# Cross-attention and FFN layer on one core: scales by PE and on-chip moves, K and V products one by one, and three kinds of transfer on ACT's queue

## The reference, cut to what matters

```
x = x + xattn(layernorm(x), ctx, mask, wq, bq, wk, bk, wv, bv, wo, bo)   # 16 batches, 112 rows, width 512; 375 context rows
x = x + ffn(layernorm(x), W1, B1, W2, B2)                                # hidden width 2048

xattn:  q = quantized_linear(x, wq) + bq        # rows of x and of wq scaled to integers up to 127
        k = ctx @ wk.T + bk ;  v = ctx @ wv.T + bv        # float32
        attn = softmax(q k.T / sqrt(32) + mask)           # 16 heads of 32
        o = attn @ v ;  out = quantized_linear(o, wo) + bo
ffn:    quantize rows, matmul with quantized W1, + B1, gelu, quantize rows, matmul with quantized W2, + B2
```

## Time and profile before

| | us |
|---|---|
| median of 3 runs | 748.97 (744.27 to 751.18) |
| the profiled execution, whole | 753.85 |
| its span, first to last instruction | 751.9 |
| mean granted clock of PE | 0.941 |
| busy: PE, DVE, ACT, POOL | 633.2, 469.8, 444.6, 300.4 |

### The profile page before, as it was taken

The page is one execution under the profiler, slowest core; times in us unless marked ns, Lnnn a source line. Parts: engine busy times, 40 slices in busy tenths (PEclk is TensorE's granted clock), DMA queues, the critical chain, the costliest instruction groups (busy, mean ns, idle before and its releaser), DMA issues.

```text
span 751.9 us, 14564 instructions
## 1 busy us (share of the span) xinstructions
PE 633.2 (84%) x4936; PEld 474.4 (63%) x4986; DVE 469.8 (62%) x1101; ACT 444.6 (59%) x1085; POOL 300.4 (40%) x555
## 2 busy tenths in 40 slices
PE   1838779979797799989699899989897999998763
PEld 1736566857665576767668677867675686766421
DVE  6635667856774295667376665468554576856763
ACT  2316555757763384949369566668584587878400
POOL 4232433453544353545452444353461333231231
PEclk9988898998998899999899999999999999999967
DMA  9985297752324425451722525324323112201321
GB/s 290 254 87 129 69 173 182 231 90 67 59 51 79 45 40 100 34 95 39 68 72 38 99 17 111 52 49 39 98 52 67 35 36 54 55 24 13 64 49 42
DMA packets 92664, 61.07 MB, mean 81 GB/s; under 512 B 69952, under 2 KB 79936, under 8 KB 91952
## 3 DMA queue, kind: packets, MB, share of 16 engines
q1 hardware_dynamic: 92592, 60.15, 41.2%
HBM read 42.09 MB, written 3.69 MB: 61 GB/s over the span
## 4 chain that ended last, share of the span: by engine, by line
PE 43%; DMA 21%; DVE 11%; SPq 9%; issue 8%; POOL 5%; ACT 1%; DVEq 0%; POOLq 0%
PE ps_ring L869 10%; PE ps_t L889 7%; PE ps_ring L855 7%; DMA oqT<-o_q 5%; PE ps_ring L933 5%; DMA q_dram<-cols 4%; PE ps_s L880 4%; PE ps_ring L945 4%; PE ps_t L902 4%; SPq L344 3%; DMA hT<-h_q 3%; DMA yqT<-y_q 2%; DMA xT<-x_q 2%; DMA q_dram<-so_col 1%; DMA b_row<-in_w2T 1%
## 5 line engine op out<-in xcount | busy, mean ns | idle before, releaser
L577 ACT ACTIVATE probs<-probs,neg_max 112x375 f32<-112x375 f32 x256 | 153.6, 602 | 36.5 <-DVE neg_max L702 36.0
L587 ACT ACTIVATE pT<-ps_t 125x336 f32<-125x336 f32 x256 | 109.0, 446 | 93.3 <-PE ps_t L889 91.6
L702 DVE CUSTOM_DVE_ANT_0 probs<-ps_s,mask_in 112x375 f32<-112x375 f32 x256 | 127.0, 543 | 56.4 <-PE ps_s L880 49.0
L889 PE MATMUL ps_t<-ident,probs 112*125 112x112 f32 x768 | 149.5, 287 | 4.4 <-ACT probs L577 2.1
L889 PEld LDWEIGHTS ps_t<-ident,probs 112*125 112x125 f32 x768 | 125.3, 199 | 36.9 <-issue 17.2
L855 PE MATMUL ps_ring<-ctx_hi,wk_hi 128*128 128x376 f32 x256 | 95.6, 373 | 29.0 <-DVE wk_lo L608 15.8
L869 PE MATMUL ps_ring<-wv_hi,ctx_hi 128*125 128x512 f32 x192 | 86.3, 449 | 2.1 <-issue 2.0
L855 PE MATMUL ps_ring<-ctx_lo,wk_hi 128*128 128x376 f32 x256 | 87.8, 343 | 0.0
L855 PE MATMUL ps_ring<-ctx_hi,wk_lo 128*128 128x376 f32 x256 | 87.6, 342 | 0.0
L463 POOL TENSOR_TENSOR ctx_lo<-ctx_in,ctx_hi 128x376 fp32r<-128x376 f32 x64 | 66.7, 1068 | 49.7 <-ACT ctx_hi L557 48.8
L945 PE MATMUL ps_ring<-w_q,hT 128*128 128x512 bf16 x207 | 65.9, 417 | 19.0 <-DMA hT<-h_q 18.2
(11 more groups left out here) (107 smaller groups left out, 1071.4 us busy)
## 6 DMA issues: line engine op xcount, KB each, us to landing
ctx_in<-in_ctxT SPq DMA_DIRECT2D x32, 375.0 KB, 6.3
h<-in_w2T SPq DMA_DIRECT2D x4, 1024.0 KB, 9.0
b_row<-in_w2T SPq DMA_DIRECT2D x4, 1024.0 KB, 9.8
xres<-in_x SPq DMA_DIRECT2D x14, 256.0 KB, 2.8
x_in<-in_x SPq DMA_DIRECT2D x16, 224.0 KB, 4.3
out<-y SPq DMA_DIRECT2D x14, 256.0 KB, 2.7
mask_in<-in_mask SPq DMA_DIRECT2D x16, 164.1 KB, 3.9
w_q<-in_w1T SPq DMA_DIRECT2D x2, 1024.0 KB, 13.9
```

Source lines behind the costliest of these rows:

```text
L577: nc.scalar.activation(probs[:, hd % SP_RING, :], probs[:, hd % SP_RING, :], ACT.Exp, scale=-1.0, bias=neg_max[:, b % 2, hd:hd + 1], accum ...
L587: nc.scalar.activation(pT[0:LR, hd % PT_RING, :], att_bank("T", b, hd, 0)[0:LR, 0:LC * N], ACT.Copy).then_inc(pT_s, 1)
L702: nc.vector.tensor_tensor_reduce(out=probs[:, hd % SP_RING, :], in0=ps_s[hd % HG][0:N, 0:L], in1=mask_in[:, b % 2, :], scale=-1.0, scalar= ...
L889: last = nc.tensor.transpose(att_bank("T", b, hd, 0)[0:LR, lc * N:(lc + 1) * N], probs[:, hd % SP_RING, lc * LR:(lc + 1) * LR], ident[0:N, ...
```

## The change

Scales. `so_store` and `so_load` go. PE transposes the broadcast column of scales against the identity into a PSUM bank (`so`), and ACT copies it to `so_row`. `xs_store` and `xs_load` go as well: PE transposes `x_s` broadcast along the free axis (`x_row`) into a `ps_t` bank, and ACT copies the row to `xs_bc`. `os_store` and `os_load` become `os_move`, one or two DMAs within SBUF from `o_s` into one of now four columns `os_col`.

Products. `k_unit` and `v_unit` issue one product each, so that other units can stand between the three. PE's total of products is the same but for the 20 new transposes.

Queues. Mask loads, residual rows and stores are issued by ACT. All five order strings are new.

```diff
 PE_UNITS = {
+    "O": ("so", each()), "x": ("x_row", each(B)),
-    "k": ("k", each(B, KC, KC)), "v": ("v", each(B, LC, KC)), "q": ("q", each(B)), "S": ("S", each(B, KC)),
+    "k": ("k", each(B, KC, 3 * KC)), "v": ("v", each(B, LC, 3 * KC)), "q": ("q", each(B)), "S": ("S", each(B, KC)),
...
 ACT_UNITS = {
+    "E": ("S", each(B, H)), "T": ("T", each(B, H)), "P": ("PV", each(B, KC)), "x": ("x_row", each(B)), "O": ("so", each()), "G": ("gelu", each(TILES, 2)),
+    "b": ("bq", each()), "m": ("mask_load", each(B)), "r": ("xres_load", each(TILES)), "s": ("store", each(TILES)),
...
 PE_ORDER = (
-    "TTTTSkdTdTdTdTdTdTddkPTkdTdTdTdTdTdkdTdTTTTTooookPkkkkkkkqSvvvvTTTTTTSuuuuuuTuTuTTTTuuuuTTTPuuuvvvTTTuvSTTTvvvvk"
+    "uuuTTkTkTkTkTkkkTkTkTkkkkkkkPkkkkgkkkkSTTkTkkkTkTkTkkkTkTkTkSTkTddddddddkTkTkTkTkkkddddddddkTkTkTkTTTTTTvvoooovv"
...
-            def so_store():
-                sp.wait_ge(wqo_stat, 5)
-                    sp.dma_start(so_dram.rearrange("(m p) -> p m", p=P), so_col[:]).then_inc(so_stored, 16)
-            def so_load():
-                sp.wait_ge(so_stored, 16)
-                sp.dma_start(so_row[:], so_dram.partition_broadcast(P)).then_inc(so_in, 16)
...
-            def xs_store(b):
-                sp.wait_ge(x_scaled, b + 1)
-                sp.dma_start(xs_dram[b % 2].unsqueeze(1), x_s[:]).then_inc(xs_stored, 16)
-            def xs_load(b):
-                sp.wait_ge(xs_stored, 16 * (b + 1))
-                sp.dma_start(xs_bc[:], xs_dram[b % 2].partition_broadcast(P)).then_inc(xs_in, 16)
...
-            def os_store(b):
+            def os_move(b):
                 sp.wait_ge(o_sc_s, b + 1)
-                sp.dma_start(os_dram[b * N:(b + 1) * N].unsqueeze(1), o_s[:]).then_inc(os_stored, 16)
-            def os_load(t):
-                sp.wait_ge(os_stored, 16 * batches_of(t))
-                wait_for(sp, y_mul, t - 1)
-                sp.dma_start(os_col[:, t % 2:t % 2 + 1], os_dram[t * P:(t + 1) * P].unsqueeze(1)).then_inc(os_in[t % 2], 16)
+                for row, end in parts(b):
+                    t = row // P
+                    wait_for(sp, y_mul, t - OS + 1)
+                    sp.dma_start(os_col[row % P:row % P + end - row, t % OS:t % OS + 1],
+                                 o_s[row - b * N:end - b * N, :]).then_inc(os_in, 16)
...
         def _(act):
+            def mask_load(b):
+                wait_for(act, masked, H * (b - 1))
+                act.dma_start(mask_in[:, b % 2, :], mask[b]).then_inc(mask_in_s[b % 2], 16)
+            def xres_load(t):
+                wait_for(act, y_res_s, t)
+                act.dma_start(xres[:], x_rows[t * P:(t + 1) * P, :]).then_inc(xres_in, 16)
+            def store(t):
+                act.wait_ge(out_s, t + 1)
+                act.dma_start(out_rows[t * P:(t + 1) * P, :], y[:, t % 2, :]).then_inc(stored[t % 2], 16)
...
+            def x_row(b):
+                act.wait_ge(xrow_pe, b + 1)
+                wait_for(act, q_mul, b)
+                nc.scalar.activation(xs_bc[:], att_bank("x_row", b)[:, 0:N], ACT.Copy).then_inc(xs_s, 1)
...
+            def x_row(b):
+                pe.wait_ge(x_scaled, b + 1)
+                bank = att_free("x_row", b)
+                nc.tensor.transpose(bank[:, 0:N], x_s[:].broadcast_to([N, P]), ident[0:N, 0:N]).then_inc(xrow_pe, 1)
...
-            def k_unit(b, g, k):
-                for t, (w_half, x_part) in enumerate(((wk_hi, ctx_hi), (wk_hi, ctx_lo), (wk_lo, ctx_hi))):
-                    last = nc.tensor.matmul(bank[:, 0:LP], w_half[:, k, cols], x_part[:, p, k, :],
+            def k_unit(b, g, step):
+                p, cols, k, part = b % 2, slice(g * P, (g + 1) * P), step // 3, step % 3
+                w_half, x_part = ((wk_hi, ctx_hi), (wk_hi, ctx_lo), (wk_lo, ctx_hi))[part]
+                last = nc.tensor.matmul(bank[:, 0:LP], w_half[:, k, cols], x_part[:, p, k, :],
```

More of the change, by code:

```diff
@@ L139 @@
 RING_USES = [use for use in turns(PE_ORDER, PE_UNITS)
-             if use[0] in ("q", "gather", "w_max") or use[0] in ("k", "v", "out_proj", "up", "down") and use[1][-1] == 0]
+             if use[0] in ("q", "gather", "w_max", "so") or use[0] in ("k", "v", "out_proj", "up", "down") and use[1][-1] == 0]
 RING_AT = {use: n for n, use in enumerate(RING_USES)}
-ATT_USES = [use for use in turns(PE_ORDER, PE_UNITS) if use[0] == "PV" or use[0] == "T" and use[1][-1] == 0]
+ATT_USES = [use for use in turns(PE_ORDER, PE_UNITS) if use[0] in ("PV", "x_row") or use[0] == "T" and use[1][-1] == 0]
 ATT_AT = {use: n for n, use in enumerate(ATT_USES)}
@@ L175, in places, with parts, parts_upto @@
     return [at] if at + N <= LEAD + OQ else [at, at - OQ]
+def parts(b):
+    cut = (b * N // P + 1) * P
+    return [(b * N, cut), (cut, (b + 1) * N)] if cut < (b + 1) * N else [(b * N, (b + 1) * N)]
+def parts_upto(b):
+    return sum(len(parts(i)) for i in range(b))
 def places_upto(b):
@@ L822, in att_free @@
                         wait_ring(pe, pT_s, H * of[0] + of[1] + 1)
+                    elif before == "x_row":
+                        wait_ring(pe, xs_s, of[0] + 1)
                     else:
@@ L844, in w_max_unit, with so_unit @@
                 nc.tensor.transpose(bank[:, 0:P], w_stat[:, 8 + which:9 + which].broadcast_to([P, P]), ident[:]).then_inc(w_max_pe, 1)
-            def k_unit(b, g, k):
-                p, cols = b % 2, slice(g * P, (g + 1) * P)
-                if k == 0:
+            def so_unit():
+                pe.wait_ge(wqo_stat, 5)
+                pe.wait_ge(ident_ready, 1)
+                bank = ring_bank("so")
+                for m in range(KC):
+                    last = nc.tensor.transpose(bank[:, m * P:(m + 1) * P], so_col[:, m:m + 1].broadcast_to([P, P]), ident[:])
+                last.then_inc(so_pe, 1)
@@ L863, in v_unit @@
                     ring_bank("v", b, lc, 0)
                 bank = bank_of("v", b, lc, 0)
-                if b == 0:
-                    pe.wait_ge(w_lo_s, KC + k + 1)
-                pe.wait_ge(ctx_lo_s, KC * b + k + 1)
-                for t, (x_part, w_half) in enumerate(((ctx_hi, wv_hi), (ctx_hi, wv_lo), (ctx_lo, wv_hi))):
-                    last = nc.tensor.matmul(bank[0:LR, :], x_part[:, p, k, rows], w_half[:, k, :],
-                                            start=(k == 0 and t == 0), stop=(k == KC - 1 and t == 2))
@@ L871, in v_unit @@
-                if k == KC - 1:
+                if part == 0:
+                    if b == 0:
+                        pe.wait_ge(w_lo_s, KC + k + 1)
+                    pe.wait_ge(ctx_lo_s, KC * b + k + 1)
+                x_part, w_half = ((ctx_hi, wv_hi), (ctx_hi, wv_lo), (ctx_lo, wv_hi))[part]
+                last = nc.tensor.matmul(bank[0:LR, :], x_part[:, p, k, rows], w_half[:, k, :],
+                                        start=(step == 0), stop=(step == 3 * KC - 1))
+                if step == 3 * KC - 1:
```

161 lines of the change are left out of this document (77 added, 84 removed).

## The result

The changed kernel takes 665.9 us, the median of 4 runs (664.13 to 667.01), beside 750.08 us for the kernel before on the same chip (744.27 to 752.14): a ratio of 0.889 with the interval 0.883 to 0.894, or 84 us. On a second chip it had 663.82 us and 0.895 (0.892 to 0.898). The forecast was 709 us with 688 as its low end: the direction was right, the gain half of what came. The profiled execution took 667.01 us with a span of 665.2 and a mean clock of 0.976.

What follows compares the result with a forecast made beforehand. The prediction took the kernel as matmul-bound on PE (43% of the chain) with DMA transfers in its way (21%). Its terms summed to -40 us, from a median of 749 to 709 us, with a range of 688 to 742.

Steps and rivals of the forecast that it cites:

- head, first scores: Start of the kernel: first scores sooner as the third batch's context load lands earlier, -5 us (-2 to -8).
- xT on PE: PE's waits for transposed x up to 164 us: the first of two goes, -6 of 9.8 us (0 to -10).
- oqT: PE's nine middle waits before the output projection: each shrinks by some 2 us, -16 of 25.5 us (-5 to -24).
- hT in the middle: PE's waits before the down products: less PE work between up and down, +2 us (-4 to +12).
- lower clock up to 700 us: PE's stretches at 1.2 GHz, mostly behind waits: half the waits gone, -8 us (0 to -20).
- ACT issues 44 transfers: Middle of the softmax: transfer issues take ACT 20 us, of which +3 us is exposed (0 to +18).
- transposes among products: PE's stream: a transpose of probs costs about 0.11 us wherever it stands, +4 us (-27 to +9).
- tail: End of the kernel: scale's DRAM trip gone, y_res about 1.5 us sooner, last hT wait whole, -1 us (-4 to +2).
- Rival A: PE's stream: transposes vanish beside the products, giving 678 us; chance 0.08.
- C: ACT's queue takes over SP's 105 us of waits, half reaching PE: slower, 761 us; chance 0.06.
- B: Transfer waits move instead of going and the clock gives nothing: 745 us, no change; chance 0.12.
- E: All transfer waits between 63 and 690 us go, and the lower clock with them: 690 us; chance 0.12.

Runs made afterwards that it cites:

- new_sp: Full change, but mask loads, residual rows and stores issued by SP again instead of ACT: ratio 0.895.
- old_os: Kernel before, old orders, with only o's row scale moved within SBUF instead of through DRAM: 699.0 us, ratio 0.945.
- old_swap: Kernel before, with the DRAM write of o's row scale put behind the transposes of o_q on SP: 778.57 us, ratio 1.048.
- ghost_behind: old_os plus an unread DRAM write of o's row scale on SP's queue, right behind the transposes of o_q: 727.82 us, ratio 0.984.
- old_xs: Kernel before, old orders, with only x's row scale transposed by PE and copied by ACT instead of through DRAM: 723.98 us, ratio 0.976.
- old_act: Kernel before, old orders, with only mask loads, residual rows and stores moved to ACT's queue: 732.2 us, ratio 0.990.
- old_ghost: old_os plus an unread DRAM write of o's row scale on SP, ahead of the move and transposes: 740.84 us, ratio 0.999.
- ghost_act: old_os plus the unread DRAM write of o's row scale, issued from ACT's queue at about the same time as in old_ghost: 747.89 us, ratio 1.012.
- new_osdram: Full change with only o's row scale through DRAM again: 689.12 us, ratio 0.927.
- new_grouped: Full change with interleaving undone, transposes and single K or V products pulled together into groups again: ratio 0.895.
- new_dram: Full change with all three scales through DRAM again and PE's row transposes removed: 755.72 us, ratio 1.024.

## Why the prediction was off by half

The sum had -40, the result is -84. By its terms:

| term | forecast | what the rows show |
|---|---|---|
| head, first scores | -5 | -13.6 (63.24 to 49.62) |
| xT on PE | -6 of 9.8 | all |
| oqT | -16 of 25.5 | all |
| yqT | -9 of 9.5 | all; 2.1 us stand in the tail |
| hT in the middle | +2 | -5.0, none left |
| probs | -6 | -1 (weight loads' wait 9.9 to 8.6) |
| lower clock up to 700 us | -8 | none left to 600 us, where 57 us had been (an estimate from the mean clocks); PE's busy time fell by 21 us |
| ACT issues 44 transfers | +3 | 0 by new_sp, which has them on SP |
| transposes among products | +4 | price of one as said (below); grouped again, no change |
| tail | -1 | +1.8 |

The two profiled spans differ by 86.7 us, and the rows split that up. The head has 13.6. Between the first scores and the last gather PE stood 64.6 us before and 10.7 after, so its waits have 53.9; the forecast had 29 for the four transfers it waits for. PE was busy 579.1 us there before and 558.1 after, at a mean clock of 0.96 and 0.99 and with some transposes more, which gives 21; the forecast had 8 for the clock. The tail takes 1.8 back.

**The step that failed** is the one under oqT on landings: that each wait "shrinks by some 2 us", since mask loads, residual rows, stores and a trip "no longer stand around it". I took the landing of 6.2 us as the price of oqT, and the shorter queue as the only reason for it to fall. It fell by 3.8 us, not by 2. It was the price of the write issued 0.7 to 2.4 us ahead: 2.4 us wherever that write was gone or stood behind (old_os, old_swap, ghost_behind, after), 4.8 to 6.5 wherever it stood ahead (old_xs, old_act, old_ghost, ghost_act, new_osdram). The rule that I weighed against my reason, that the DMAs of all issuers share the same 16 engines (the Trainium skill, DMA: Bandwidth & Descriptors, Issuing engines are not separate DMA queues), held: the move to ACT's queue gives 1% in the old orders and nothing in the new. The consequence that I drew from it, a landing that stays at 6.2 us, was wrong. The write had held up what was issued behind it from either queue (old_ghost, ghost_act), and the change took the write away. Everything that it held up had its own term, each cut by hand to a part: ctx_in in the head (-5, "it took 13 us in a stretch full of small packets"), xT, oqT, the clock that follows PE's waits. All came whole.

**A wait that the sum lacked** is DVE's. The sum has PE's waits and SP's, and not those of DVE for the scale (23.0 us in 6 at y_res, shown above); out_proj's bank and the whole FFN of a tile stand behind y_res. In the order of before it had no price of its own, as old_ghost shows, where it is gone and the time is the same. In old_swap, where it is 50.6 us and oqT is early, the time rose by 35.

**The head.** Right that ctx_in of the third batch ends the wait and not xs_bc, wrong that its 13 us would stay near. Issued 6.5 us sooner, its first half landed within 4.6 us (37.49 to 42.12), and the second held nobody.

**The transposes** were right. In the new order, in order of time on PE:

```profile
300.49 0.26 PE L908 MATMUL ps_t<-ident,probs 112*125 112x112 f32 x1
300.52 0.42 PE L873 MATMUL ps_ring<-ctx_lo,wk_hi 128*128 128x376 f32 x1
300.78 0.33 PE L873 MATMUL ps_ring<-ctx_hi,wk_lo 128*128 128x376 f32 x1
300.95 0.34 PE L873 MATMUL ps_ring<-ctx_hi,wk_hi 128*128 128x376 f32 x1
```

A transpose with a K product takes 0.29 us (300.49 to 300.78), a K product alone 0.17: 0.12 for the transpose, as in the earlier trace rows. Rival A, by which it vanishes, falls, and new_grouped shows that where the transposes stand is worth nothing either way.

**The tail** kept its length within the range of its term, but y_res did not come sooner. The read that it had waited for is gone, and DVE's h_quant of the tile ahead, which the forecast had about 1 us later, ends 2.8 us later behind the gather (14.7 us instead of 11.9), so that y_res starts at 14.6 as it had at 14.7.

**The rivals.** C (ACT's queue stands in SP's waits) did not come: with these transfers back on SP's queue, new_sp has the same time. B did not: hT's waits in the middle went too. E was the nearest, all transfer waits between 63 and 690 gone and the clock with them, at 690; I gave it 0.12, still kept the head at -5 in it, and its 9 + 4 + 5 leave the clock 5 at most. The range of 688 to 742 missed by 22 us because every landing had been cut on its own, as if they had no common cause, so that the far end was never all of them together.

**How the gain divides.** On the chip of the single edits the full change gains 10.5 points (0.895). Alone, o's scale has 5.5, x's 2.4 and the queue 1.0; the three together have 8.6, which leaves 1.9 for the new orders with wo's scale. Turned round, in the new orders the queue is worth 0, spreading the transposes 0, and the three transports 13 points (0.895 to 1.024) against trips at the places of new_dram. What stays open is what makes single values into DRAM slow inside the chip, and how the last 10 points of new_dram divide between x's and wo's scales.

## What to carry to other kernels

Price a transfer by what it does to its neighbours, not by who waits for it: when transfers that should be quick land late in the median, look for one small write ahead of them and take it away alone. A column of values, one per partition, should not be written to DRAM on a busy path; move it within SBUF, turn it by PE, or make it a row first. Before changing an order or a queue to hide a wait, issue the suspected transfer unread in a version that does not need it: here one such run told the write from the wait for its data, which moving the write (old_swap) had mixed up.

## What the runs showed of the hardware

- 112 values of 4 bytes from 112 partitions: 6.6 us to DRAM, 1.7 us within SBUF. As one row out of one partition such a write to DRAM completed in 1.1 us and changed no time (0.945 with and without).
- While the slow write is under way, transfers issued after it complete late, also when it came from another engine's queue (ghost_act): on-chip moves 6.3 us instead of 1.7, transposes 5.8 instead of 2.4, context loads 6.9 instead of 4.1 in the median (old_ghost beside old_os).
- 41 us of a 742 us program hung on sixteen such writes. PE's longer waits behind them also brought its clock down: the mean is 0.966 in old_os and 0.949 in old_ghost, so by an estimate from these means some 48 and 75 us of the two spans stood at the lower level.
